# First attention layer of an eight-layer kernel: input in four transfers, products inside the norm, the split on three engines, the first head's loads reordered, and score operands of 65 rows

## The reference

```python
def _L0_attn_ref(x, w_qkv, w_proj, b_proj, rel_bias_table):
    B, N, C = x.shape                  # 4, 512, 128
    H = rel_bias_table.shape[1]        # 16 heads
    D = C // H                         # 8
    qkv = (x @ w_qkv.T).reshape(B, N, 3, H, D)
    q, k, v = (jnp.transpose(qkv, (2, 0, 3, 1, 4))[i] for i in range(3))
    scores = jnp.einsum('bhqd,bhkd->bhqk', q, k) * D ** (-0.5)
    scores = scores + compute_bias(N, N, rel_bias_table)
    attn = jax.nn.softmax(scores, axis=-1)
    out = jnp.einsum('bhqk,bhkd->bhqd', attn, v)
    return jnp.transpose(out, (0, 2, 1, 3)).reshape(B, N, C) @ w_proj.T + b_proj
```

## Time and profile before

| | before |
| --- | --- |
| time, median of 3 runs (lowest to highest) | 2320.22 us (2318.97 to 2323.26) |
| the profiled execution's own time | 2328.94 us |
| its span | 2327.1 us |
| mean granted TensorE clock | 0.887 |
| busy: PE / DVE / ACT / POOL | 1866.4 / 1692.1 / 1070.6 / 837.5 us |

### The profile page before, as it was taken

One profiled execution on the slowest core, in us unless ns is written; L12 is line 12 of the kernel. 1 busy time (PEld: TensorE's weight loads), 2 busy tenths in 40 slices (PEclk: granted clock), 3 DMA queues, 4 the chain that ended last, 5 costly groups with the idle time before them and its releaser, 6 DMA issues. The chain is left out here.

```text
span 2327.1 us, 46335 instructions
## 1 busy us (share of the span) xinstructions
PE 1866.4 (80%) x16408; PEld 1291.3 (55%) x16408; DVE 1692.1 (73%) x4008; ACT 1070.6 (46%) x2009; POOL 837.5 (36%) x637
## 2 busy tenths in 40 slices
PE   4999995688888885579999667887887759997756
PEld 2666663355555553367777534454554448886444
DVE  3899997676666676688999873988998772224574
ACT  1777773355554441134444333555555413332542
POOL 3000002875555511133444344444554217921111
PEclk8999997899999997779999965999998659998787
DMA  3111112000000000010000074444544350000000
GB/s 111 34 46 45 45 41 70 17 17 17 17 18 17 17 18 5 1 24 24 13 22 23 0 215 114 149 147 142 158 147 142 90 192 26 19 8 7 1 1 21
DMA packets 127630, 129.08 MB, mean 55 GB/s; under 512 B 75117, under 2 KB 103635, under 8 KB 126698
## 3 DMA queue, kind: packets, MB, share of 16 engines
q1 hardware_dynamic: 127466, 126.91, 18.4%
HBM read 78.59 MB, written 40.81 MB: 51 GB/s over the span
## 5 line engine op out<-in xcount | busy, mean ns | idle before, releaser
L2727 ACT ACTIVATE l2a_pr<-l2a_ps_s,l2a_nm 128x512 f32<-128x512 f32 x256 | 173.8, 685 | 130.1 <-DVE l2a_nm L2650 124.0
L454 ACT ACTIVATE l0a_pr<-l0a_sm,l0a_nm 128x512 f32<-128x512 f32 x256 | 185.1, 724 | 87.6 <-DVE l0a_nm L367 84.7
L367 DVE CUSTOM_DVE_ANT_0 l0a_sm<-l0a_ps_s,l0a_tb 128x512 f32<-128x512 f32 x256 | 176.1, 689 | 24.4 <-PE l0a_ps_s L522 9.1
L530 PE MATMUL l0a_ps_p<-top_c_ident,l0a_pr 128*128 128x128 f32 x1024 | 171.2, 291 | 0.0
L2650 DVE TENSOR_REDUCE l2a_nm<-l2a_ps_s 128x2 f32<-128x1024 f32 x128 | 156.7, 1224 | 4.4
L1612 POOL TENSOR_TENSOR l1f_h<-l1f_lm,l1f_sg 128x512 f32<-128x512 f32 x72 | 92.5, 1284 | 184.7 <-DVE l1f_lm L1676 184.7
L2657 DVE STREAM_TRANSPOSE l2a_tt<-l2a_pr 128x1024 f32<-128x1024 f32 x128 | 158.0, 1234 | 0.7 <-ACT l2a_pr L2727 0.6
L530 PEld LDWEIGHTS l0a_ps_p<-top_c_ident,l0a_pr 128*128 128x128 f32 x1024 | 109.7, 143 | 59.0 <-issue 45.8
L1738 ACT ACTIVATE l1f_csb<-l1f_ps_c,l1f_b3e 128x512 f32<-128x512 f32 x128 | 88.1, 688 | 108.2 <-PE l1f_ps_c L1524 107.9
L1991 ACT ACTIVATE l2f_h<-l2f_ps_h 128x512 f32<-128x512 f32 x128 | 76.4, 598 | 132.3 <-PE l2f_ps_h L1524 126.0
L1958 DVE SCALAR_TENSOR_TENSOR l2f_acc<-l2f_ps_y,l2f_comb,l2f_acc 128x128 f32<-128x128 f32 x112 | 31.6, 344 | 133.9 <-PE l2f_ps_y L2032 133.9
(11 more groups left out here) (531 smaller groups left out, 5120.4 us busy)
## 6 DMA issues: line engine op xcount, KB each, us to landing
l_qband<-l2a_staged SPq DMA_DIRECT2D x16, 768.0 KB, 15.7
l2a_qb<-l_qband SPq DMA_DIRECT2D x16, 768.0 KB
l2a_sb<-l_pband SPq DMA_DIRECT2D x32, 384.0 KB
l0a_tb<-l_bias SPq DMA_DIRECT2D x16, 448.0 KB
l2a_ks<-l_k SPq DMA_DIRECT2D x16, 384.0 KB
l_pband<-l2a_pr SPq DMA_DIRECT2D x32, 192.0 KB, 8.0
l_pband<-l2a_pr SPq DMA_DIRECT2D x32, 144.0 KB, 3.0
l2f_upw<-in_L_ffn_up_weights SPq DMA_DIRECT2D x9, 512.0 KB, 9.6
```

The source lines that it names most:

```text
L367: v.tensor_tensor_reduce(sm[j % 4][:, :], ps_s[j % 2][:, :], tb[slot][:, off:off + N][:, ::-1], -1.0, 3e38, ALU.add, ALU.min, nm[:, j % 4: ...
L454: a.activation(pr[j % 4][:, :], sm[j % 4][:, :], ACT.Exp, bias=nm[:, j % 4:j % 4 + 1], scale=-1.0).then_inc(m["p_ready"], 1)
L530: last = pe.transpose(ps_p[j % 4][:, tile(k)], pr[j % 4][:, tile(k)], ident[:, :])
L2727: a.activation(pr[slot][:, 2 * (g % 2) + u, :], ps_s[g % 2][:, u, :], ACT.Exp, bias=nm[:, g % 2, u:u + 1], accum_out=rs[:, n % 2, 2 * (g % ...
```

## The change

Five edits, all in the two functions and in what calls the first.

1. The block of `load` is gone. x comes in four transfers, one per batch, with a semaphore each, at the head of the first layer's SP stream; the constants needed late follow it and are waited for at the end of the layer. ACT issues the transfers of the bias table, the one-hot matrix, two constants and the weights.
2. PE computes the bias table first, then turns the weights, and multiplies a batch as soon as it is turned. Turned batches and V products use two banks each.
3. The split: ACT takes the middle cast, POOL only subtracts, the residual goes into a ring of four (`sm`, idle at that time). ACT, in place of DVE, copies the bias table and V out of PSUM.
4. The first head's bias rows are loaded right behind the stores of the table, its q as soon as q is stored, its k as soon as k is stored.
5. Score operands get 65 rows (`FULL_ROWS`, `L2_ROWS`) in both layers; rows 48 (51 in the later layer) to 64 are zero on both sides. In the first layer POOL and DVE fill the tiles with zeros once at the start; in the later layer SP copies zeros in with four transfers before its first head, the heads lie in two tiles, both at partition 0, and the first score of a tile waits for three transfers rather than one.

```diff
+FULL_ROWS = P // 2 + 1
-def load(nc, s, xs, x, consts):
...
-            sp.dma_start(xs[:, :, :], xv).then_inc(loaded, 16)
-            for k, a in consts.items():
-                sp.dma_start(c[k][:, :], a).then_inc(loaded, 16)
-            sp.wait_ge(loaded, 16 * (1 + len(consts)))
...
+SPLIT_ORDER = ((0, 0), (1, 0), (0, 1), (1, 1), (0, 2), (0, 3), (1, 2), (1, 3))
...
-        qs = [s.sb(f"qs{i}", [KROWS, T * P], BF16) for i in range(2)]
-        ks = [s.sb(f"ks{i}", [KROWS, T * P], BF16) for i in range(2)]
+        qs = [s.sb(f"qs{i}", [FULL_ROWS, T * P], BF16) for i in range(2)]
+        ks = [s.sb(f"ks{i}", [FULL_ROWS, T * P], BF16) for i in range(2)]
...
+        ps_z = [ps_p[2], ps_p[0]]
+        ps_v = [ps_p[3], ps_p[1]]
...
             @block.sync
             def _(sp):
+                for b in range(B):
+                    sp.dma_start(xs[:, b * NT:(b + 1) * NT, :], xv[:, b * NT:(b + 1) * NT, :]).then_inc(x_loaded[b], 16)
...
-                sp.wait_ge(m["parts_stored"], 16 * 2 * B)
-                sp.wait_ge(m["tb_stored"], 16)
-                load(0, 0)
+                sp.wait_ge(m["tb_stored"], 16)
+                load_bias(0, 0)
+                sp.wait_ge(m["rows_zero"], 4)
+                sp.wait_ge(m["q_stored"], 16 * B)
+                load_parts(sp, qs[0], qk3[0], 0, turn_loaded[0], True)
+                sp.wait_ge(m["k_stored"], 16 * B)
+                load_parts(sp, ks[0], qk3[1], 0, turn_loaded[0], False)
                 load(1, 1)
...
             @block.gpsimd
             def _(g):
+                for rows in qs:
+                    g.memset(rows[:, :], 0.0).then_inc(m["rows_zero"], 1)
...
-                    g.tensor_copy(mid, res[n % 2][:, :]).then_inc(m["mid_ready"], 1)
+                for n, (i, b) in enumerate(SPLIT_ORDER):
+                    g.wait_ge(m["mid_ready"], n + 1)
+                    g.tensor_tensor(parts[:, i, 2, b * N:(b + 1) * N], sm[n % 4][:, :], parts[:, i, 1, b * N:(b + 1) * N],
+                                    ALU.subtract).then_inc(m["lo_ready"], 1)
...
             @block.vector
             def _(v):
...
+                statistics(0)
+                statistics(1)
+                normalize_rows(0)
+                statistics(2)
+                normalize_rows(1)
+                statistics(3)
+                residual(0)
+                normalize_rows(2)
+                residual(1)
+                normalize_rows(3)
+                for n in range(2, 2 * B):
+                    residual(n)
...
             @block.scalar
             def _(a):
...
+                a.dma_start(table[:, :], w["rel_bias_table"]).then_inc(m["t_loaded"], 16)
+                a.dma_start(onehot[:, :], c["t5_onehot"]).then_inc(m["t_loaded"], 16)
...
+                for n in range(4, 2 * B):
+                    high(n)
+                    middle(n - 1)
...
             @block.tensor
             def _(pe):
...
+                pe.wait_ge(m["va_ready"], B)
...
 FROWS = KROWS + 3
+L2_ROWS = P // 2 + 1
+PAD = L2_ROWS - FROWS
-        qs = s.sb("qs", [2 * (P // 2), T * P], BF16)
+        qs = [s.sb(f"qs{i}", [L2_ROWS, T * P], BF16) for i in range(2)]
...
+                    sp.dma_start(qs[i][FROWS:, :].rearrange("p (r c) -> p r c", c=P), zero_rows[:, :].unsqueeze(1).broadcast_to([PAD, T, P])).then_inc(head_loaded[i], 16)
+                    sp.dma_start(ks[i][FROWS:, :, :].rearrange("p v (r c) -> p (v r) c", c=P), zero_rows[:, :].unsqueeze(1).broadcast_to([PAD, 2 * T, P])).then_inc(head_loaded[i], 16)
...
-                        pe.wait_ge(head_loaded[h % 2], 16 * (HEAD_LOADS * (h // 2 + 1) + 1))
+                        pe.wait_ge(head_loaded[h % 2], 16 * (HEAD_LOADS * (h // 2 + 1) + 3))
```

More of the change, by code:

```diff
@@ L192, in constants, with constant_tiles @@
     return c
[L196 to L208 removed]
+def constant_tiles(s, consts):
+    return {k: s.sb("c_" + k, list(a.shape)) for k, a in consts.items()}
 def store(nc, s, xs, out):
@@ L341, in _ @@
                 ch = Chain(v, m["dve"])
[L342 to L347 removed]
+                for rows in ks:
+                    v.memset(rows[:, :], 0.0).then_inc(m["rows_zero"], 1)
@@ new lines, in statistics, with normalize_rows, residual @@
+                def statistics(b):
+                    v.wait_ge(x_loaded[b], 16)
+                    ln.statistics(v, ch, b, lambda t: xs[:, b * NT + t, :])
+                def normalize_rows(b):
+                    if b >= 2:
+                        v.wait_ge(m["t_ready"], b - 1)
+                    ln.normalize(v, ch, b, lambda t: xs[:, b * NT + t, :], lambda t: zb[:, b % 2, t, :])
+                    ch.wait()
+                    v.sem_inc(m["zb_ready"], 1)
+                def residual(n):
+                    i, b = SPLIT_ORDER[n]
@@ L448, in _, with middle @@
                                  scale=SCALE if i == 0 else 1.0).then_inc(m["hi_ready"], 1)
+                def middle(n):
+                    i, b = SPLIT_ORDER[n]
+                    a.wait_ge(m["res_ready"], n + 1)
+                    a.copy(parts[:, i, 1, b * N:(b + 1) * N], sm[n % 4][:, :]).then_inc(m["mid_ready"], 1)
+                copy_z(0)
+                high(0)
+                high(1)
+                copy_z(1)
+                middle(0)
+                high(2)
+                middle(1)
+                high(3)
+                copy_z(2)
+                copy_z(3)
+                middle(2)
+                for n in range(4, 2 * B):
+                    high(n)
+                    middle(n - 1)
+                middle(2 * B - 1)
+                for b in range(B):
+                    a.wait_ge(m["v_ps"], b + 1)
+                    a.copy(va[:, b * NT:(b + 1) * NT, :, :],
+                           ps_v[b % 2][:, :].rearrange("p (t h d) -> p t h d", t=NT, d=HD)).then_inc(m["va_ready"], 1)
                 def exp(n, j):
@@ L486, in _ @@
                 tile = lambda t: slice(t * P, (t + 1) * P)
-                pe.wait_ge(m["w_loaded"], 48)
+                pe.wait_ge(m["t_loaded"], 32)
+                for i in range(2):
+                    pe.matmul(ps_p[i][0:HEADS, :], table[:, :], onehot[:, i * N:(i + 1) * N], start=True, stop=True).then_inc(m["tb_ps"], 1)
+                pe.wait_ge(m["ident_loaded"], 16)
+                pe.wait_ge(m["w_loaded"], 32)
                 for i in range(4):
```

147 lines of the change are left out of this document (79 added, 68 removed).

## The result

| | before | changed |
| --- | --- | --- |
| median, first comparison | 2319.59 us (4 runs) | 2283.36 us (2281.95 to 2289.92, 4 runs) |
| ratio, 95% interval | | 0.985 [0.9823, 0.9878] |
| profiled execution, span | 2327.1 us | 2281.1 us |
| first maximum of the loop on DVE | 55.6 us | 41.2 us |
| from there to unit 16 | 21.6 us | 16.2 us |

The changed kernel is 36 us faster; 29 were forecast. A second comparison gave 0.9812 [0.979, 0.9834], 2281.29 us against 2321.7. In the two profiles the first layer accounts for 14.4 + 5.4 + 17.1 - 0.2 = 36.7 us of the 46.0 by which the spans differ, the third attention layer for 9.1. The median moved by 36 and not by 46: before's profiled execution was 9 us above its median.

A forecast was written before the change was run, and what follows sets the result against it. Bound: a chain of hand-overs until 54.81 us, then PE in the first layer's loop, DVE 7% behind. Gains 17.8 + 2 + 9.5 + 0 = 29.3 us off the median 2320.22 leave 2291; own range 2283 to 2299, full range 2278 to 2305.

The forecast's parts named there:

- the forecast's own case: Whole kernel: the terms hold as summed, 2291 us, own range 2283 to 2299; chance 0.70.
- The start: First layer up to its first score: score at 37 us instead of 54.81, 17.8 us gained, between 12 and 21.
- q's loads and the bias rows have gone by then: First layer's start: when the last store lands at 29.7 us, only k's issue of 1.89 us remains before the wait.
- Rival B: First layer's start saves less, stores and ACT setting the pace: first score about 45, kernel 2299 us; chance 0.08.
- The ramp: First layer's scores at 1.2 GHz, 54.81 to 69 us: fewer weight-load pauses gain 2 us, from 0 to 3.8.
- 65 rows: First layer's loop: padded score operands remove weight-load pauses, DVE then sets the pace; 9.5 us gained, from 5 to 12.6.
- rival A: Padding to 65 rows does nothing, so ramp and loop gains go: kernel 2302 us; chance 0.13.
- it idles for 2.5 us ahead of the maximum: First layer's steady loop: DVE's idle in 58 us, taken as 12.6 us over 293 us, three quarters of it gained.
- The third attention layer: Later layer with 65 rows: shorter pauses gain 2 us, zero fills cost 2; net 0, from -4 to +6.
- Rival C: First layer's loop: PE idle drops the clock to 1.2 GHz; at 25 cold groups the kernel ends at 2336; chance 0.04.

## Why the prediction was right

The time lies within the range, and the forecast's own case came true: no rival did. But 2283.4 is at the very edge of that case's 2283 to 2299, the second comparison's 2281.3 below it, and the terms were off by 3 to 8 us each.

- *The start*, 17.8 us forecast, 14.4 measured. First product near 11 (11.8) and last low part near 27 (28.8) held roughly; 1.8 us of the miss is there. k's issue began 32.03 - 28.77 = 3.3 us behind the last low part and not 2.6: "q's loads and the bias rows have gone by then" was wrong, they stood in SP's stream behind the last store and ahead of k. The landing of k was mis-sized: 5 us forecast, 6.5 measured, at the first head's own transfers. Rival B, the stores and ACT as the pace, did not come: its first score was at 45.
- *The ramp*, 2 forecast and 3.8 as its upper bound, 5.4 measured. The term counted the pauses and not the clock, which rises 10 us sooner without them (16.8 and 6.6 us after the first score).
- *65 rows*, 9.5 forecast and 12.6 as its bound, 17.1 measured. That the pause goes with the row count, and that 65 counts as 85 and 128 do, was right: 64 rows have it, 65 do not. So "TensorEngine Tiling (Array Packing)" of the Trainium skill, "Tiling Modes", "Key Properties", stands here, and rival A does not. The rule of the Trainium skill, "TensorE: Matmul & The Clock Gate", Part 3, "What overlaps and what doesn't", would have had pauses left between 65 and 128 rows, and none is in the trace. The term failed in its size, at "it idles for 2.5 us ahead of the maximum": DVE's shown idle time was taken for all that it waited. Its instructions overlap by 0.09 us when nothing holds them, so part of each wait is recorded as busy. All idle time in the 58 us was 4.2 before and is 3.7 now, 0.35 and 0.29 us a group: only 0.06 of the 0.27 that a group lost was shown as idle. By pitches (201.66 to 206.13 in the trace of after, the same instruction one group on) a group takes 4.47 us, against 4.75 before, and 0.28 x 60 groups gives 17. PE's side was mis-sized too: a unit of 0.65 us and not 0.50, so in the steady loop PE is busy for 91% and not 70 to 80, and DVE for 94% and not 97 or more. As DVE sets the pace, this cost the forecast nothing.
- *The third attention layer*, 0 forecast, between -4 and +6: 9 in the one pair of profiles, 0 to 9 by all runs. Not settled.
- *Rival C*, the clock, is out: 1.00 with PE busy for 91% of the time.

The first three misses, +3.4, -3.4 and -7.6 us, add up to -7.6, as much as the median came out below the forecast. That the start and the ramp cancel is luck, and so is that the loop's miss left the time just inside the range.

## What to carry over

Look at the weight loads' own idle times before calling a full PE bound by matmuls: operands of 48 or 64 rows among ones of 128 made the loads stand still for 0.4 us a unit here, zero rows up to 65 removed it, and 64 did not. What that is worth depends on the next engine: PE's unit fell by 0.25 us, the loop by 0.07 a unit, as DVE was next. To see what an engine would gain when the one ahead of it gets faster, add up the pitches of its instructions (start to start where nothing waits), not its busy time and not its idle time. Once a bound has moved, ask at once what the new one holds: two small edits to DVE's part of the loop gave another 30 us.

## What was not expected of the hardware

- POOL's fill of two tiles of 65 x 2048 bf16 took 3.54 us, DVE's of one, as 4-byte words, 0.91. Beside POOL's fills four DVE row operations took 6.98 us in place of 1.11.
- TensorE's clock rose 6.6 us after the first score with 65 rows and 16.8 with 48, though PE was recorded as busy for 10.50 of 10.50 us ahead of the late rise.
- The same start had the clock's rise at 15 to 16 us in most profiles and at 21 in one; there the last low part ended 2 us later and the first score came 3 later.
- One zero fill from 256-byte pieces kept SP's queue for 4.75 us; the one of the same size before it took 0.80. In all eleven profiles it was 3.3 to 4.75 and 0.80.
